# Normalising after the value product in a grouped attention layer, and a new order of its transposes

## The reference

```python
q = hidden_state @ Wq + bq          # 32 heads of 16
k = encoder_hidden_state @ Wk + bk  # 8 heads of 16
v = encoder_hidden_state @ Wv + bv
scores = einsum('bkgld,bksd->bkgls', q, k) / sqrt(16) + mask
attn = softmax(scores, axis=-1)     # over 128 keys
out = einsum('bkgls,bksd->bkgld', attn, v)
x = out @ Wo + bo + hidden_state
return layer_norm(x, eps=1e-6) * gamma + beta
```

## Time and profile before

| what | value |
|---|---|
| median of 3 runs | 2668.98 us (2668.42 to 2671.52) |
| profiled execution | 2673.65 us, span 2671.9 us |
| PE busy | 2474.4 us (93%) |
| DVE busy | 1230.2 us (46%) |
| ACT busy | 1086.5 us (41%) |
| POOL busy | 1105.6 us (41%) |
| mean granted clock of PE | 0.970 |

### The profile page before, as it was taken

The page is one execution under the profiler, slowest core; times in us unless marked ns, Lnnn a source line. Parts: engine busy times, 40 slices in busy tenths (PEclk is TensorE's granted clock), DMA queues, the critical chain, the costliest instruction groups (busy, mean ns, idle before and its releaser), DMA issues.

```text
span 2671.9 us, 48698 instructions
## 1 busy us (share of the span) xinstructions
PE 2474.4 (93%) x18464; PEld 2072.0 (78%) x18464; DVE 1230.2 (46%) x3295; ACT 1086.5 (41%) x3705; POOL 1105.6 (41%) x1972
## 2 busy tenths in 40 slices
PE   7999998999997788857988899999899999899999
PEld 5887886888886666747877788888788888688887
DVE  4555564323225766644445533332355555432322
ACT  4555563111117777745556411111355555311111
POOL 2454446400035898963544560003244444640000
PEclk9999999999999999978999999999899999999999
DMA  4112212211112222221222231112211211321100
GB/s 155 57 57 70 90 49 92 63 48 48 56 61 85 82 92 83 66 84 64 72 96 92 76 122 48 48 40 61 78 49 49 89 48 49 98 63 41 48 32 16
DMA packets 110326, 181.30 MB, mean 68 GB/s; under 512 B 7888, under 2 KB 43408, under 8 KB 109072
## 3 DMA queue, kind: packets, MB, share of 16 engines
q1 hardware_dynamic: 110096, 178.19, 20.3%
HBM read 132.02 MB, written 46.14 MB: 67 GB/s over the span
## 4 chain that ended last, share of the span: by engine, by line
PE 80%; POOL 7%; ACT 6%; DVE 4%; issue 2%; DMA 1%; SPq 0%; DVEq 0%; POOLq 0%; ACTq 0%
PE banks L317 71%; PE banks L453 5%; ACT plain_high L700 4%; POOL plain_high L1274 4%; PE banks L480 3%; DVE neg_max L954 1%; PE banks L504 1%; DVE rounded_work L1052 1%; DVE plain_high L950 0%; POOL rounded_high L308 0%; POOL rounded_low L308 0%; PE banks L442 0%; DVE rounded_work L1026 0%; POOL rstd L1289 0%; ACT plain_high L684 0%
## 5 line engine op out<-in xcount | busy, mean ns | idle before, releaser
L317 PE MATMUL banks<-rounded_work,rounded_low 128*128 128x512 f32 (+1 forms) x2688 | 535.2, 357 | 58.3 <-issue 35.3
L1274 POOL TENSOR_SCALAR plain_high<-plain_high,inv_sum 128x128 f32<-128x128 f32 (+1 forms) x1024 | 386.7, 401 | 392.4 <-DVE inv_sum L972 391.3
L317 PEld LDWEIGHTS banks<-rounded_work,rounded_low 128*128 128x128 f32 x2688 | 447.4, 200 | 125.4 <-issue 53.6
L317 PE MATMUL banks<-rounded_work,rounded_high 128*128 128x512 f32 (+1 forms) x2400 | 488.2, 357 | 8.6 <-DMA rounded_work<-ctx_split 6.4
L929 ACT ACTIVATE plain_work<-banks,columns 128x512 f32<-128x512 f32 x192 | 132.5, 690 | 865.2 <-PE banks L317 865.2
L317 PEld LDWEIGHTS banks<-rounded_work,rounded_high 128*128 128x128 f32 x2400 | 399.1, 192 | 76.6 <-issue 9.4
L1250 DVE CAST rounded_work<-plain_work 128x512 fp32r<-128x512 f32 x192 | 102.0, 531 | 689.3 <-ACT plain_work L929 678.1
L317 PE MATMUL banks<-rounded_low,rounded_work 128*128 128x512 f32 x1728 | 413.1, 391 | 0.0
L317 PE MATMUL banks<-rounded_high,rounded_work 128*128 128x512 f32 (+1 forms) x1728 | 395.2, 381 | 0.0
L317 PEld LDWEIGHTS banks<-rounded_low,rounded_work 128*128 128x128 f32 x1728 | 322.1, 188 | 69.0 <-issue 3.0
L317 PEld LDWEIGHTS banks<-rounded_high,rounded_work 128*128 128x128 f32 x1728 | 314.1, 192 | 60.5 <-issue 1.4
(11 more groups left out here) (101 smaller groups left out, 3058.0 us busy)
## 6 DMA issues: line engine op xcount, KB each, us to landing
plain_work<-x SPq DMA_DIRECT2D x96, 256.0 KB, 2.8
plain_work<-mlp_w SPq DMA_DIRECT2D x96, 256.0 KB, 2.7
rounded_work<-ctx_split SPq DMA_DIRECT2D x24, 1024.0 KB, 5.9
u<-plain_work SPq DMA_DIRECT2D x48, 256.0 KB, 3.0
plain_work<-u SPq DMA_DIRECT2D x12, 1024.0 KB, 7.2
x<-plain_work SPq DMA_DIRECT2D x48, 256.0 KB, 2.2
plain_work<-attention_w SPq DMA_DIRECT2D x44, 256.0 KB, 2.7
plain_work<-inputs_t SPq DMA_DIRECT2D x8, 1024.0 KB, 7.8
```

Of the source, the lines that this page charges most:

```text
L317: mm = pe.matmul(dst, lhs(i), rhs(j), start=first and n == 0, stop=last and n == 2, skip_group_check=True)
L1274: last = pool.tensor_scalar(part, part, inv_sum[:, R % 2, r, g:g + 1], 1.0, ALU.mult, ALU.mult)
```

## The change

In the grouped layer alone, the exponentials are no longer multiplied by the reciprocals before they are turned; the value product is made of the plain exponentials and is divided afterwards. For that, DVE takes the reciprocals spread to the shape of the product (`inv_wide`: each sum repeated 16 times, two instructions of 128x128), PE turns the two into the free half of the value product's bank, DVE copies that half to SBUF (`by_head`) and multiplies the product by it. POOL then adds the bias and makes the high and the low part (`pool_heads`), in place of `act_heads`, `dve_heads` and `pool_norm`. ACT copies one of the four turned banks instead of two, DVE three. The transposes are issued a bank at a time with other products between them, the exponentials of a round now come behind the turned bank 3 of the round before, and both halves of the queries have moved. At the end, the third layer's first rows are turned ahead of the last output product, and its mask and split rows are made ahead of the last moments; the last `dve_again` comes behind the third layer's first queries.

```diff
+        def pe_turn_bank(pe, y, p, k, r):
             R = y.round(p, k)
             pr = prob(y)[R % 2]
+            key = ("T", R, r)
+            dst = begin(pe, key)
+            if y.kind == GQA:
+                pe.wait_ge(exped, 4 * (R - y.r0) + r + 1)
+            else:
+                pe.wait_ge(normed, 4 * plain_round(y, R) + r + 1)
+            for t in range(4):
+                mm = pe.transpose(dst[:, t * P:(t + 1) * P], pr[:, r, t * P:(t + 1) * P], ident[:, :])
+            mm.then_inc(filled_by(key), 1)
...
             dst = begin(pe, key)
-            for r in range(4):
-                wait_evac(pe, ("T", R, r))
             for i in range({LATENT: 4, GQA: 1, CROSS: 2}[y.kind]):
                 wait_evac(pe, ("V", y.n, p, i))
...
+            if y.kind == GQA:
+                pe.wait_ge(g_inverted, R - y.r0 + 1)
+                for i in range(2):
+                    pe.transpose(dst[:, (2 + i) * P:(3 + i) * P], inv_wide[:, i, :], ident[:, :])
+            for r in range(4):
+                wait_evac(pe, ("T", R, r))
...
-                    wait_evac(pe, ("O", y.round(p, k)))
+                    if y.kind == GQA:
+                        pe.wait_ge(heads_ready, y.round(p, k) - y.r0 + 1)
+                    else:
+                        wait_evac(pe, ("O", y.round(p, k)))
...
                 pe_scores(pe, y, p, 1)
-                pe_turn_probs(pe, y, p, 0)
+                pe_turn_bank(pe, y, p, 0, 0)
                 if more:
                     pe_turn_x(pe, y, p + 1)
+                pe_turn_bank(pe, y, p, 0, 1)
                 if p:
                     pe_out(pe, y, 2 * p - 1)
+                pe_turn_bank(pe, y, p, 0, 2)
+                pe_turn_bank(pe, y, p, 0, 3)
                 pe_attend(pe, y, p, 0)
+                pe_scores(pe, y, p, 2)
+                pe_turn_bank(pe, y, p, 1, 0)
+                if more:
+                    pe_queries(pe, y, p + 1, 0)
+                pe_turn_bank(pe, y, p, 1, 1)
                 if more:
                     pe_keys(pe, y, p + 1, 0)
-                pe_scores(pe, y, p, 2)
-                pe_turn_probs(pe, y, p, 1)
-                if more:
-                    pe_queries(pe, y, p + 1, 0)
+                pe_turn_bank(pe, y, p, 1, 2)
+                pe_turn_bank(pe, y, p, 1, 3)
                 pe_attend(pe, y, p, 1)
                 pe_scores(pe, y, p, 3)
-                pe_turn_probs(pe, y, p, 2)
+                pe_turn_bank(pe, y, p, 2, 0)
+                if more:
+                    pe_queries(pe, y, p + 1, 1)
+                pe_turn_bank(pe, y, p, 2, 1)
                 if more:
                     pe_values(pe, y, p + 1, 0)
+                pe_turn_bank(pe, y, p, 2, 2)
+                pe_turn_bank(pe, y, p, 2, 3)
                 pe_attend(pe, y, p, 2)
                 if more:
                     pe_scores(pe, y, p + 1, 0)
-                pe_turn_probs(pe, y, p, 3)
+                pe_turn_bank(pe, y, p, 3, 0)
+                pe_turn_bank(pe, y, p, 3, 1)
                 pe_out(pe, y, 2 * p)
+                pe_turn_bank(pe, y, p, 3, 2)
+                pe_turn_bank(pe, y, p, 3, 3)
                 pe_attend(pe, y, p, 3)
-                if more:
-                    pe_queries(pe, y, p + 1, 1)
+            pe_turn_x(pe, L[2], 0)
             pe_out(pe, y, B - 1)
...
+            def quarter(p, k, early, mid, late):
+
+                n = p * y.per_pair + k + 1
+                for r in range(4):
+                    if r == 3:
+                        early()
+                    if r:
+                        dve_probs(dve, y, p, k, r - 1)
+                    if n < y.rounds:
+                        dve_max(dve, y, n // 4, n % 4, r)
+                mid()
+                R = y.round(p, k)
+                dve.wait_ge(exped, 4 * (R - y.r0 + 1))
+                for i in range(2):
+                    by_row = row_sum[:, R % 2, :, 2 * i:2 * i + 2].unsqueeze(3).broadcast_to([P, 4, 2, 16])
+                    last = dve.reciprocal(inv_wide[:, i, :].rearrange("p (r e d) -> p r e d", r=4, e=2), by_row)
+                last.then_inc(g_inverted, 1)
+                late()
+                wait_filled(dve, ("O", R))
+                dve.tensor_copy(by_head, bank(("O", R))[:, 2 * P:4 * P]).then_inc(g_moved, 1)
+                wait(dve, heads_ready, R - y.r0 - 1)
+                dve.wait_ge(g_moved, R - y.r0 + 1)
+                dve.tensor_tensor(o_tmp[:, k % 2, :], bank(("O", R))[:, 0:2 * P], by_head, ALU.mult).then_inc(evac_of(("O", R)), 1)
...
+                quarter(p, 0, rows_in, nothing, rows_out)
+                quarter(p, 1, nothing, lambda: queries(0), keys)
+                quarter(p, 2, nothing, lambda: queries(1), nothing)
+                quarter(p, 3, nothing, nothing, lambda: dve_out(dve, y, 2 * p))
+            dve_mask(dve, L[2], 0)
+            dve_x(dve, L[2], 0, 0)
+            dve_x(dve, L[2], 0, 1)
             dve_again(dve, y, B - 2)
             dve_out(dve, y, B - 1)
-            dve_again(dve, y, B - 1)
...
+        def pool_heads(pool, y, p, k):
+            R = y.round(p, k)
+            b, s = of_round(y, k)
+            n, o, ot = R - y.r0, o_tmp[:, k % 2, :].rearrange("p (c n) -> p c n", c=2), heads_t(y)[:, b]
+            wait_evac(pool, ("O", R))
+            for i in range(2):
+                last = pool.tensor_scalar(o[:, i, :], o[:, i, :], col(y, 8 + 2 * s + i), 1.0, ALU.add, ALU.mult)
+            last.then_inc(o_biased, 1)
+            pool.wait_ge(o_biased, n + 1)
+            pool.tensor_copy(ot[:, 0, 2 * s:2 * s + 2, :], o).then_inc(o_hi, 1)
+            pool.wait_ge(o_hi, n + 1)
+            pool.tensor_tensor(ot[:, 1, 2 * s:2 * s + 2, :], o, ot[:, 0, 2 * s:2 * s + 2, :].bitcast(F32), ALU.subtract).then_inc(heads_ready, 1)
...
-                pool_norm(pool, y, p, 1)
                 if p:
                     pool_again(pool, y, 2 * p - 2)
                     pool_root(pool, y, 2 * p - 1)
-                pool_norm(pool, y, p, 2)
+                pool_heads(pool, y, p, 0)
                 if p:
                     pool_again(pool, y, 2 * p - 1)
                 pool_bias(pool, y, 2 * p)
+                pool_heads(pool, y, p, 1)
                 split_tile(pool, ("a", 2), 2 * p)
-                pool_norm(pool, y, p, 3)
+                pool_bias(pool, y, 2 * p + 1)
+                pool_heads(pool, y, p, 2)
                 split_tile(pool, ("a", 2), 2 * p + 1)
-                pool_bias(pool, y, 2 * p + 1)
-                if more:
-                    pool_norm(pool, y, p + 1, 0)
                 pool_root(pool, y, 2 * p)
+                pool_heads(pool, y, p, 3)
```

More of the change, by code:

```diff
@@ L122, in build @@
         gamma, beta = work(plain, 26, D), work(plain, 28, D)
+        o_tmp, inv_wide = work(plain, 30, 2, 2 * P), work(plain, 25, 2, P)
+        by_head = work(plain, 62, 2 * P)
         unit_g, unit_c = work(plain, 44, 2, D), work(plain, 28, 2, D)
@@ L237, in col, with plain_round @@
             return cols[:, y.n, i:i + 1]
+        def plain_round(y, R):
+            return R if y.n == 0 else R - L[1].rounds
         def of_round(y, k):
@@ L695, in act_exp @@
             else:
-                act.wait_ge(maxed, 4 * (R if y.n == 0 else R - L[1].rounds) + r + 1)
+                act.wait_ge(maxed, 4 * plain_round(y, R) + r + 1)
             for g in range(y.segs):
@@ L866, in act_gqa @@
                 more = p + 1 < PAIRS
-                def inputs():
-                    if more:
-                        act_x(act, y, p + 1, 0)
-                        act_x(act, y, p + 1, 1)
-                act_round(act, y, p, 1, (p, 0), inputs)
-                act_heads(act, y, p, 0)
+                for r in range(3):
+                    act_exp(act, y, p, 0, r)
+                if more:
+                    act_x(act, y, p + 1, 0)
+                    act_x(act, y, p + 1, 1)
+                act_exp(act, y, p, 0, 3)
+                act_probs(act, y, p, 0, 3)
+                for r in range(3):
+                    act_exp(act, y, p, 1, r)
+                if more:
+                    act_queries(act, y, p + 1, 0)
+                act_exp(act, y, p, 1, 3)
                 if more:
                     act_keys(act, y, p + 1, 0)
-                act_round(act, y, p, 2, (p, 1), nothing)
+                act_probs(act, y, p, 1, 3)
+                for r in range(3):
+                    act_exp(act, y, p, 2, r)
                 if more:
-                    act_queries(act, y, p + 1, 0)
-                act_heads(act, y, p, 1)
-                act_round(act, y, p, 3, (p, 2), nothing)
+                    act_queries(act, y, p + 1, 1)
+                act_exp(act, y, p, 2, 3)
                 if more:
                     act_values(act, y, p + 1, 0)
-                act_heads(act, y, p, 2)
-                act_round(act, y, p + 1, 0 if more else None, (p, 3), nothing)
-                act_heads(act, y, p, 3)
-                if more:
-                    act_queries(act, y, p + 1, 1)
```

(19 more changed lines are left out.)

46 lines of the change are left out of this document (8 added, 38 removed).

## The result

The changed kernel takes 2748.1 us (median of 4 runs, 2745.76 to 2751.85) against 2670.25 us for the kernel before on the same chip: a ratio of 1.0291, 95% interval 1.0273 to 1.0309, slower. Its profiled execution took 2747.5 us with a span of 2745.7, against 2673.65 and 2671.9: 73.9 us more. The forecast was 2765 in a range of 2695 to 2805.

What follows compares the result with a forecast made beforehand. POOL was taken to bound the grouped layer, then the DVE-PE chain. The profiled 2673.65 plus net 66.4 (layer +73.1, handover -6.7) plus clock 30 gives 2770; the median, 4.7 below, 2765, range 2695 to 2805.

Steps and rivals of the forecast that it cites:

- the walk through the rounds: Grouped layer, four rounds of a pair stepped through DVE and PE: 16.6 + 12.2 + 14.0 + 12.3 = 55.1 us against 44.5.
- the clock's cost: Rounds with 6 to 7 us without big products: half of 31, 15, lose 2.0 us each, +30 (0 to 65).
- POOL stops being the bound, DVE and PE take turns: Grouped layer: POOL's 22 us a pair go, DVE-PE turns cost more; 2765 us, own range 2730 to 2800, chance 0.62.
- The faster rival: Grouped layer: DVE's own work becomes the bound, a pair 42.1 us or 36 with cheap reciprocals; about 2645, chance 0.09.
- Wide reciprocals: DVE's two 128x128 reciprocals a round: 1.04 us each by slope, 2.0 us a round; high end 1.9 each.
- The low end, 0.3: DVE's wide reciprocals cost only another pass over 128 columns, 0.3 us; as a rival 2720 or 2690, chance 0.16.
- Copy and multiplication: DVE's extra steps on the spread product, 256 columns from PSUM: 0.4 to 0.5 us each, 1.0 with one wait.
- The odd batch's output product: First round on PE: waits for POOL's root and heads, 4.4 + 2.0 = 6.5 us after DVE's start.
- Start: Grouped layer's start: exponentials come behind the values, first value product ends about 829 instead of 826.5, +2.5 us.
- The layer's end: Grouped layer's last value product filled at 1246.7 instead of 1173.6 us, +73.1.
- Handover: Last value product to the third layer's keys: 9.8 us instead of 16.5, -6.7.
- the 9 to 12 that I had named as a sign: Handover sign that the forecast is right: third layer's keys 9 to 12 us behind the last value product.

Runs made afterwards that it cites:

- experiments 3: Changed kernel with all four transposes of the exponentials ahead of the big products in each round, ACT and DVE taking inputs behind the turned banks: 2698.3 us.
- 7: Changed kernel with transposes first and ACT's exponentials of the next round ahead of or between queries, keys and values, not all behind them: 2664.15 us.
- experiment 4: Kernel before with the handover's order alone (third layer's first rows turned and split early, last moments later): 2659.33 us, ratio 0.9961.
- Experiment 1: Changed kernel with one 128x16 reciprocal a round, spread by two broadcast copies, in place of two 128x128 reciprocals: 2713.52 us.
- Experiment 6: Changed kernel with idle products on PE before its wait for the reciprocals and POOL's fourth-round heads ahead of the even batch's root: 2702.97 us.
- 2: Changed kernel with POOL's heads of the fourth round ahead of the root of the even batch, nothing else: 2732.48 us.
- Experiment 8: Changed kernel with transposes first, exponentials ahead, one narrow reciprocal spread by copies, and POOL's fourth-round heads ahead of the root: 2653.06 us.
- experiment 10: Experiment 8's kernel with DVE's split of the next pair's rows moved behind the last minimum and the copy of turned bank 2: 2629.26 us.

## Why the prediction was right, and where its terms were off

The sign, the mechanism and the place were right; the sum was 23 us too high for the profiled execution (2770 against 2747.5) and 17 for the median (2765 against 2748.1). That it came so near is in part luck: the walk through the rounds was too long, and the clock's cost, which was added once at the end, lay inside the measured rounds.

- **POOL stops being the bound, DVE and PE take turns.** Right, and shown: experiments 3 and 7 took back 84 us by order alone, where the change had cost 78; beside experiment 4 some 5 us are still missing. Experiment 1 gave 34.6 of the 36.3 us it took from DVE. The faster rival asked that PE's big products run while DVE has its minima. In the change they don't; in 7 they do, and the pair fell to some 44 us, near that rival's 42.1.
- **Wide reciprocals**: 1.04 us each by the slope of the earlier trace rows, 0.92 measured, the two in 1.68 to 1.76. A little high: 31 x 0.3 = 9 us. The low end, 0.3, was wrong. By 246 ns for 16 elements (experiment 1) and 920 for 128, one costs 6.0 ns.
- **Copy and multiplication**: 0.42 and 0.43 us, with the wait 0.95: right (1.0).
- **The rounds.** In the order first, second, third, fourth, filled bank to filled bank, the walk gave 15.6, 13.1, 14.35 and 12.05 us; between the starts of value products the trace has 14.7, 12.5, 15.0 and 12.5. The sum, 55.1 against 54.9 (55.8 in the mean of five pairs), is closer than the terms deserve: the walk had no clock in it and the measured pair has. In the third round I can follow it link by link in the chain above: 14.35 charged, about 0.75 us too much for PE's products and 0.3 for the reciprocals, and some 1.7 us of lower clock on top make the 15.0 measured. Queries and values follow each other in 2.87 and 2.63 us where I had charged 3.1 and 2.87, because a matmul group's time in a timeline, as in the earlier trace rows, runs past the start of the next one (the queries of 1011.91 take 3.11 us, and the turns behind them start at 1014.86, 0.16 us before their end); the reciprocals take 1.68 for 2.05. Against that the turned reciprocals and the value product take 0.66 and 1.86 at the lower clock (0.50 over the value product).
- **The odd batch's output product** waited for root and heads as predicted: root from 1036.96, 4.4 us, heads 2.0 (1041.35 to 1043.37), product at 1043.46. It began 5.6 us after DVE's start (1037.86) and not 6.5, since the root had started 0.9 before it.
- **Start**: the first value product ended at 828.92 us against 826.53, +2.4, predicted +2.5. **The layer's end**: the walk without clock said 1246.7, the last value product ended at 1255.84. So of the 30 us set aside for the clock only 9 came on top.
- **The clock: about the size set aside, at other places; the walk under it was the term that was mis-sized.** The layer's granted clock fell from 0.92 to 0.83. I had it strike the big products in half of the rounds, 15, 2.0 us each: an estimate of mine, and no run shows that term. The runs showed this in its place. It strikes mostly the small ones: in the pairs of 54.9 us, in three rounds of four the value product takes 1.94 us at a granted clock of 0.50 for 1.08 at 1.00 (the turned reciprocals 0.66 for 0.41, scores up to 1.67 for 1.00), while the big products behind them are back at 3.12, 2.88 and 2.97 (granted clock 1.00). From these rows about 1.1 us in each of three rounds, and up to 1 us more where scores lie on the chain: 3.3 to 4.3 a pair, 26 to 33 us in 31 rounds. That is an estimate. Big products were struck too, but seldom: queries in the two pairs of 57.3 us (3.79 us for 3.12 at 886.72, granted clock 0.80) and one output product (5.46 us at 1210.43, granted clock 0.50), some 7 us more. In all that is the size forecast or a little over it, and it was hidden in the total by a walk some 3.5 to 4 us a pair too long. Experiment 6 against 2 shows 29.5 us won back by idle products alone, once POOL's wait is away.
- **What sets the clock is not shown.** Behind PE's stretches of turns and idling the value products of 1008.29, 1023.32 and 1035.86 take 1.94 us, each at a granted clock of 0.50. But the value product of 1050.60, behind the same eight turns and 2.95 us of idling as that of 1035.86, takes 1.08 us at 1.00. And no run here tells turns from idling: experiment 7 with its 16 turns in a row, and waits for DVE of up to 2.9 us, has 0.97 in 940 to 1100 us, which speaks against turns alone being the cause.
- **Handover**: predicted 16.5 to 9.8, measured 12.35, just outside the 9 to 12 that I had named as a sign. The output product took 4.56 us at the lower clock (0.64 over it) for 3.0, and POOL's two scalings 1.87 us for 0.73. With the 9 us of the layer's end that makes the keys 78.1 later, where 66.4 and a clock of 30 had been forecast. Behind them nothing was lost: the third layer's second keys are 76.8 later and the end 73.8.

## What to carry to other kernels

When an engine that bounds a stage is relieved, ask before all what order then binds the others: here 22 us a pair were taken from POOL and 10 to 11 were lost to two engines in turn, each idle for the other. Put what a slower consumer waits for (turned banks, exponentials) ahead of large work that nobody awaits yet, on every engine that feeds the chain, and not on PE alone. Price an edit by the chain it stands on, and read the chain anew after each step, since one edit was worth 34.6, 6.7 or 18.5 us by what stood beside it, and moving two instructions behind one copy and one minimum was worth 23.8. And when one change carries two, time them apart: the handover's order alone gave 11 us.

## What the runs showed that I had not expected

- **Some instructions of POOL and DVE took longer side by side.** A copy of 128x128 from SBUF to SBUF took 0.18 us, but over 1 us while POOL ran TENSOR_TENSOR. Experiment 8, DVE once beside POOL and once without, then the POOL row that lies over the slow one:

```profile
986.39 2.14 DVE L1212 COPY plain_work<-inv_sum 128x128 f32<-128x128 f32 x2
...
997.44 0.36 DVE L1212 COPY plain_work<-inv_sum 128x128 f32<-128x128 f32 x2
```

```profile
985.94 1.27 POOL L316 TENSOR_TENSOR rounded_low<-plain_work,rounded_low 128x512 fp32r<-128x512 f32 x1
987.17 1.27 POOL L1335 TENSOR_TENSOR plain_work<-plain_work 128x512 f32<-128x512 f32 x1
```

  The casts of the changed kernel's handover do the same (first with POOL's TENSOR_TENSOR of 1257.90 and 1259.24 running, then without one), and POOL's scaling beside DVE's cast and subtraction took 1.87 us for two, against 0.73 at 1041.35:

```profile
1258.01 1.44 DVE L1076 CAST rounded_work<-plain_work 128x512 fp32r<-128x512 f32 x1 [0.92 <-ACT plain_work L793]
...
1261.04 0.41 DVE L1076 CAST rounded_work<-plain_work 128x512 fp32r<-128x512 f32 x1
```

```profile
1257.90 1.26 POOL L1367 TENSOR_TENSOR plain_work<-plain_work 128x512 f32<-128x512 f32 x1
...
1260.55 1.87 POOL L1423 TENSOR_SCALAR plain_work<-plain_work,columns 128x128 f32<-128x128 f32 x2
```

  Experiment 8's two copies took 2.14 or 2.15 us in four rounds, of which this is one, 1.45 in a fifth, and 0.36 to 0.56 elsewhere: 21.2 us for all 64, where experiment 1 has 12.0. No run took POOL's work away to test it, so the cause is read from the overlap and not shown.
- **A short wait sometimes cost twice, but no length of it says when.** In experiment 8, 2.85 us of idle before the output product went with 1.6 us more for the product itself (4.58 for 3.0, granted clock 0.62). In the changed kernel 2.4 to 2.65 us before the same product went with nothing (2.97 to 3.02), and so did 0.88 us in experiment 10 (2.97). Yet 0.79 us before the queries of experiment 10 went with 3.13 us in one pair and with 4.63 in the next. The cost has to be read from the trace, pair by pair.
